# Two attention layers on one core: a gathered column that ScalarE fetches row by row, and codes of a picked column in two versions instead of seven

## The reference, cut to what matters

```python
edge_index = jnp.stack([src, dst])
x = _layernorm(x + _L0_gnn_ref(x, edge_index, ...))      # edge MLP, segment_max
x = _layernorm(x + _L1_gnn_ref(x, edge_index, ...))      # two attention layers

def _gat_conv(x, W, att_src, att_dst, bias, src, dst, n_nodes):
    h = x @ W
    a_src = h @ att_src
    a_dst = h @ att_dst
    e = a_src[src] + a_dst[dst]
    e = jnp.where(e > 0, e, NEG_SLOPE * e)
    m = jax.ops.segment_max(e, dst, num_segments=n_nodes)
    ex = jnp.exp(e - m[dst])
    denom = jax.ops.segment_sum(ex, dst, num_segments=n_nodes)
    alpha = ex / denom[dst]
    msg = alpha[:, None] * h[src]
    out = jax.ops.segment_sum(msg, dst, num_segments=n_nodes)
    return out + bias
```

## Time and profile before

| | |
|---|---|
| median of three executions | 5880.39 us (5874.37 to 5883.29) |
| profiled execution | 5872.45 us, its span 5871.2 us |
| busy share of the span | PE 84%, POOL 75%, DVE 70%, PEld 52%, ACT 45% |
| first attention layer, POOL's gathers | 2189.3 to 3896 us |
| second attention layer, POOL's gathers | 4055.9 to 5764 us |
| POOL gathers of both layers (L545) | 2712 |
| picked columns, codes, one-hot pieces of both layers | 384, 2688, 2688 |

### The profile page before, as it was taken

One profiled execution on the slowest core, in us unless ns is written; L12 is line 12 of the kernel. 1 busy time (PEld: TensorE's weight loads), 2 busy tenths in 40 slices (PEclk: granted clock), 3 DMA queues, 4 the chain that ended last, 5 costly groups with the idle time before them and its releaser, 6 DMA issues.

```text
span 5871.2 us, 119756 instructions
## 1 busy us (share of the span) xinstructions
PE 4931.6 (84%) x29429; PEld 3060.9 (52%) x29429; DVE 4098.0 (70%) x10676; ACT 2658.7 (45%) x8225; POOL 4399.4 (75%) x4585
## 2 busy tenths in 40 slices
PE   3688888888888729999999999943999999999991
PEld 2566666666666525555555555522555555555550
DVE  4344454444445448888888888864888888888886
ACT  2233333333333235555555555533555555555554
POOL 7777777777777677777777777767777777777775
PEclk6899999999999959999999999976999999999995
DMA  6677777777777724444444444432444444444442
GB/s 157 187 219 217 215 223 216 217 219 217 220 217 216 202 59 120 123 124 122 124 125 124 125 124 124 125 92 63 124 123 124 124 125 124 124 124 121 125 125 83
DMA packets 808269, 874.81 MB, mean 149 GB/s; under 512 B 133438, under 2 KB 635185, under 8 KB 807818
## 3 DMA queue, kind: packets, MB, share of 16 engines
q0 software_dynamic: 146016, 295.63, 19.7%
q1 hardware_dynamic: 390298, 361.70, 18.8%
q10 hardware_dynamic: 271504, 213.69, 13.9%
HBM read 536.74 MB, written 331.81 MB: 148 GB/s over the span
## 4 chain that ended last, share of the span: by engine, by line
POOL 51%; issue 21%; DVE 9%; PE 7%; DMA 6%; ACT 3%; DVEq 0%; POOLq 0%; SPq 0%; ACTq 0%
POOL ring_a L545 25%; POOL ring_a L485 22%; DMA ring_a<-H_table,src_i 6%; PE ps L1417 5%; DVE ring_b L1120 5%; ACT ring_a L746 2%; POOL ring_a L512 2%; POOL ad_edges L520 2%; POOL P_compact L498 1%; PE ps L1311 1%; DMA ring_a<-Q_table,src_i 1%; DVE ring_a L1074 1%; PE ps L1321 1%; DVE gz L1104 1%; DVE ring_b L1074 0%
## 5 line engine op out<-in xcount | busy, mean ns | idle before, releaser
L545 POOL DMA_INDIRECT ring_a<-H_table,src_i x2712 | 2588.2, 954 | 826.9 <-issue 755.9
L1417 PE MATMUL ps<-work,ring_a 128*128 128x390 bf16 x10752 | 1867.3, 330 | 238.5 <-DVE ring_a L1074 234.9
L485 POOL DMA_INDIRECT ring_a<-Q_table,src_i x1501 | 1432.8, 955 | 461.0 <-issue 453.0
L1417 PEld LDWEIGHTS ps<-work,ring_a 128*128 128x128 bf16 x10752 | 1015.8, 98 | 1065.2 <-DVE ring_a L1074 387.7
L1417 PE MATMUL ps<-work,ring_b 128*128 128x390 bf16 x8064 | 1407.7, 329 | 0.0
L638 ACT ACTIVATE code<-src_row,code_bias 128x128 int16<-128x128 int32 x2676 | 829.5, 389 | 1214.2 <-DVE ring_b L1074 1152.0
L1120 DVE SCALAR_TENSOR_TENSOR ring_b<-ring_b,gw,ring_a 128x129 f32<-128x129 f32 x3124 | 1092.0, 350 | 120.4 <-ACT ring_a L746 104.2
L948 DVE TENSOR_TENSOR_SCAN work<-ring_b,work,ps 128x512 f32<-128x512 bf16 x390 | 498.4, 1278 | 951.8 <-PE ps L1321 911.1
L1417 PEld LDWEIGHTS ps<-work,ring_b 128*128 128x128 bf16 x8064 | 787.0, 98 | 559.7
L746 ACT ACTIVATE ring_a<-ring_a,gw 128x129 f32<-128x129 f32 x3126 | 959.3, 390 | 0.0
L1074 DVE TENSOR_TENSOR ring_a<-code,ps 128x896 bf16<-128x896 int16 x1536 | 944.1, 615 | 1.2 <-issue 0.3
(11 more groups left out here) (267 smaller groups left out, 3625.2 us busy)
## 6 DMA issues: line engine op xcount, KB each, us to landing
run_sum<-ring_b SPq DMA_DIRECT2D x388, 520.0 KB
work<-P_compact SPq DMA_DIRECT2D x1563, 64.0 KB
ring_b<-rank_rows ACTq DMA_DIRECT2D x194, 512.0 KB, 5.2
run_max<-tab_flat ACTq DMA_DIRECT2D x194, 512.0 KB
one_rows<-H_table SPq DMA_DIRECT2D x3840, 0.5 KB
ring_a<-H_table,src_i POOLq DMA_INDIRECT x2712
src_row<-in_srcL SPq DMA_DIRECT2D x384, 64.0 KB, 3.0
ring_a<-Q_table,src_i POOLq DMA_INDIRECT x1501
```

What stands on the lines that cost most here:

```text
L485: pool.indirect_dma_start(out=q_ring[:, g % RING, j - j0, :], out_offset=None, in_=Q_table, in_offset=bass.IndirectOffsetOnAxis(ap=srcT_i[ ...
L545: pool.indirect_dma_start(out=h_ring[:, g % RING1, j - j0, :], out_offset=None, in_=H_table, in_offset=bass.IndirectOffsetOnAxis(ap=src_i[ ...
L1417: m = tensor.matmul(ps[parity][:, 0:3 * W], lhsT=hot_space[c // 4][:, c % 4, k - k0, :], rhs=split[:, k, :, :].rearrange("p s f -> p (s f) ...
```

## The change: what it does

Everything is in the two attention layers.

1. **A column by ACT.** `by_few` holds every 17th group (19, 36, ... 189; 11 a layer). One of its columns is no longer gathered by POOL. In a turn of 17 groups ACT loads the column's source numbers to `few_src` (`list_few`), then after its scaling in each of 16 groups reads two times 4 numbers into registers and issues 8 row DMAs into `few_rows` (`fetch_few`), and in the 17th moves the column to the ring (`move_few`). VectorE waits for it in the group it belongs to (`few_moved`). In one group a layer (87) both `by_row` and `by_few` apply, and POOL gathers 5 columns.
2. **Two codes for seven.** The places of blocks now stand in four PSUM banks (banks 2 to 5): bank 2 as before by TensorE, banks 3 to 5 by 21 small VectorE memsets at the start of each layer (`bf16_pair` is the bit pattern of two equal bf16 values). They hold the places 0 to 27 in units of 128, so piece c compares code c // 4 with bank c % 4, and ACT makes 2 codes instead of 7.
3. **Order.** On ACT the codes of g + 3 are made behind the row fetches, once for the group. At the layer's start ACT waits for the stored table, and VectorE's wait for `proj_tab` stands ahead of its other waits, before the memsets.

```diff
-        blocks_ps = ps[2][:, :].bitcast(BF16)[:, 0:PIECE * P].rearrange("p (k e) -> p k e", e=P)
+        blocks_ps = [ps[2 + v][:, :].bitcast(BF16)[:, 0:PIECE * P].rearrange("p (k e) -> p k e", e=P) for v in range(4)]
...
+        FEW_TURN, FEW = 17, 8
+        FEW_TURNS = (NPICK - 2) // FEW_TURN
+        by_few = [FEW_TURN * (i + 1) + 2 for i in range(FEW_TURNS)]
...
-        by_dma = [(j0, j1 - (g in picks) - (g in by_row)) for g, (j0, j1) in enumerate(groups1)]
+        by_dma = [(j0, j1 - (g in picks) - (g in by_row) - (g in by_few)) for g, (j0, j1) in enumerate(groups1)]
...
                 def code_of(g):
-                    code_row(NQPICK + layer * NPICK + picks[g])
-
+                    at = NQPICK + layer * NPICK + picks[g]
+                    scalar.wait_ge(row_landed[row_slot[at]], row_value[at])
+                    scalar.wait_ge(hot_made, at * PIECES)
+                    scalar.activation(code[:, 0, :], src_row[:, row_slot[at], :], ACT.Identity, bias=code_bias[:, 0:1])
+                    scalar.activation(code[:, 1, :], src_row[:, row_slot[at], :], ACT.Identity, bias=code_bias[:, 4:5]).then_inc(coded, 1)
+
+                def list_few(turn):
+
+                    g = by_few[turn]
+                    j = groups1[g][1] - 2 - (g in by_row)
+                    scalar.dma_start(few_src[:, :], t["srcL"][j:j + 1, :]).then_inc(few_listed, 16)
+
+                def fetch_few(turn, p):
+
+                    if p == 0:
+                        scalar.wait_ge(few_listed, 16 * (layer * FEW_TURNS + turn + 1))
+                        if layer or turn:
+                            scalar.wait_ge(few_moved, 16 * (layer * FEW_TURNS + turn))
+                    for e0 in range(p * FEW, min((p + 1) * FEW, P), 4):
+                        _, row = nc.values_load_multi_w_load_instructions(
+                            few_src[0:1, e0:e0 + 4], engines=[scalar.engine], min_val=0, max_val=NP - 1,
+                            skip_runtime_bounds_check_because="sources are numbers of nodes")
+                        for d in range(4):
+                            scalar.dma_start(few_rows[e0 + d:e0 + d + 1, :], H_table[bass.ds(row[d], 1), :]).then_inc(few_landed[layer], 16)
+
+                def move_few(turn):
+
+                    g = by_few[turn]
+                    scalar.wait_ge(few_landed[layer], 16 * P * (turn + 1))
+                    scalar.wait_ge(summed, layer * L + groups1[g - RING1][1])
+                    scalar.dma_start(h_ring[:, g % RING1, G1 - 2 - (g in by_row), :], few_rows[:, :]).then_inc(few_moved, 16)
+
+                list_few(0)
+                scalar.wait_ge(h_stored, 16 * B * (layer + 1))
...
-                        if g + 3 in picks and i == G1 - 1:
-                            code_of(g + 3)
+                    turn, p = divmod(g, FEW_TURN)
+                    if p == 0 and 1 <= turn <= FEW_TURNS:
+                        move_few(turn - 1)
+                    if p == 0 and 1 <= turn < FEW_TURNS:
+                        list_few(turn)
+                    if p >= 1 and turn < FEW_TURNS:
+                        fetch_few(turn, p - 1)
+                    if g + 3 in picks:
+                        code_of(g + 3)
...
             for layer in range(2):
+                vector.wait_ge(proj_tab, 3 * B * (layer + 1))
+                for v in range(1, 4):
+                    for k in range(PIECE):
+                        vector.memset(ps[2 + v][:, k * P // 2:(k + 1) * P // 2], bf16_pair((v * PIECE + k) * P)).then_inc(dve.up(), 1)
...
-                    vector.tensor_tensor(hot_space[c // 4][:, c % 4, 0:k1 - k0, :], code[:, c:c + 1, :].to_broadcast([P, k1 - k0, P]),
-                                         blocks_ps[:, 0:k1 - k0, :], ALU.is_equal).then_inc(hot_made, 1)
+                    vector.tensor_tensor(hot_space[c // 4][:, c % 4, 0:k1 - k0, :],
+                                         code[:, c // 4:c // 4 + 1, :].to_broadcast([P, k1 - k0, P]),
+                                         blocks_ps[c % 4][:, 0:k1 - k0, :], ALU.is_equal).then_inc(hot_made, 1)
...
+                    if g in by_few:
+                        vector.wait_ge(few_moved, 16 * (layer * FEW_TURNS + by_few.index(g) + 1))
```

More of the change, by code:

```diff
@@ L1 @@
+import struct
 from contextlib import ExitStack
@@ L36, in cut, with bf16_pair @@
     return groups
+def bf16_pair(value):
+    high = struct.unpack("<I", struct.pack("<f", float(value)))[0] >> 16
+    return struct.unpack("<f", struct.pack("<I", high * 65537))[0]
 def totals(slots, amounts):
@@ L98, in edge_network @@
         one_src, one_rows = sb("one_src", [1, P], I32), sb("one_rows", [P, W])
+        few_src, few_rows = sb("few_src", [1, P], I32), sb("few_rows", [P, W])
         x_sb = sb("x_sb", [P, NB, F])
@@ L208, in edge_network @@
         assert SHARE * (TURN - 1) >= P and all(g in picks for g in by_row) and TURN % RING1 == 0
+        FEW_TURN, FEW = 17, 8
+        FEW_TURNS = (NPICK - 2) // FEW_TURN
+        by_few = [FEW_TURN * (i + 1) + 2 for i in range(FEW_TURNS)]
+        assert FEW * (FEW_TURN - 1) >= P and all(g in picks for g in by_few)
         q_value = totals([g % RING for g in range(NG)], [16 * (j1 - j0 - (g in q_picks)) for g, (j0, j1) in enumerate(groups)])
@@ L246, in edge_network @@
         one_ready, one_landed = sem("one_ready"), [sem(f"one_rows{i}") for i in range(2)]
+        few_listed, few_moved, few_landed = sem("few_listed"), sem("few_moved"), [sem(f"few_rows{i}") for i in range(2)]
         tabs_stored, compact_zeroed, p_scattered, ranks_stored = (
@@ L1048, in vector_program @@
             for layer in range(2):
+                vector.wait_ge(proj_tab, 3 * B * (layer + 1))
+                for v in range(1, 4):
+                    for k in range(PIECE):
+                        vector.memset(ps[2 + v][:, k * P // 2:(k + 1) * P // 2], bf16_pair((v * PIECE + k) * P)).then_inc(dve.up(), 1)
                 vector.wait_ge(ad_loaded, 16 * (layer + 1))
                 vector.wait_ge(adx_loaded, 16 * (layer + 1))
-                vector.wait_ge(proj_tab, 3 * B * (layer + 1))
                 vector.wait_ge(proj_copied, 2 * B * (layer + 1))
@@ L1407, in tensor_program @@
                 for k in range(PIECE):
-                    tensor.transpose(blocks_ps[:, k, :], block_at[:, k, :], ident_b[:, :]).then_inc(blocks_put, 1)
+                    tensor.transpose(blocks_ps[0][:, k, :], block_at[:, k, :], ident_b[:, :]).then_inc(blocks_put, 1)
                 def pick(parity, added, hot):
```

## The result

The changed kernel took 5849.94 us in the median of five executions (5849.85 to 5855.10), the kernel before 5875.80 (5873.03 to 5883.29): a ratio of 0.9956, 95% interval 0.9945 to 0.9966, so 20 to 32 us faster. The forecast was 5852.7, 27.7 us under a before of 5880.39; between the two medians measured here lie 25.9 us. The profiled execution took 5855.1 us and was the slowest of its five.

What follows compares the result with a forecast made beforehand. POOL's gather rate was taken as the bound: 22 gathers at 1.259 us save 27.7 us and all other terms cost nothing, so 5880.39 - 27.7 = 5852.7 us, range 5842 to 5882.

Steps and rivals of the forecast that it cites:

- What bounds it: In the layers' steady part POOL's gather rate sets the 8.68 us a group; TensorE needs 8.2 us, VectorE 8.0.
- The gathers that go: On POOL in both layers, 22 fewer gathers at 1.259 us with gap save 27.7 us; added DMAs make none dearer.
- Will POOL be held back: POOL's wait for sums of the group three before has 7 us of room; fewer gathers use 1.26 or 2.5.
- ACT's new work: On ACT, 352 steps of 8 row fetches, 4.0 to 4.9 us each, fit 5.2 us of room: cost nothing.
- the first rival: Slow register loads push ACT's fetch step past 5.2 us, so ACT's round is the bound: 116 to about 500 slower; 13%.
- ACT becomes the bound: In the layers, ACT's own round becomes the group's time: 116 us slower, or about 500 with longest loads; chance 13%.
- SP becomes the bound: On SP's queue, each ACT issue holds up SP's for its whole 0.23 us: 350 us slower, 6230; chance 5%.
- The rest: VectorE's comparisons and wait for the moved column, some 2 us of memsets, ACT's list load and table wait: cost nothing.
- What would show each step: Signs in the trace: 2690 gathers at 1.26 us, 8.61 us a group, ACT's waits and load prices, SP still waiting.

## Why the prediction was right

**What bounds it.** Right. POOL's waits are its gap and no more, before and after, and a kernel that takes more gathers away ran down to TensorE's 8.16 us.

**The gathers that go.** Right, 22 x 1.26 us: 27.7 forecast, 25.9 measured, with 27.7 in the interval. The column left out with no replacement gave the same 0.9953 as the changed kernel on the same chip. The edge MLP's gathers were a fair row for what other DMAs do to POOL's price.

**Will POOL be held back.** Right: no wait over 0.3 us.

**ACT's new work.** The result, nothing, was right; the account behind it was wrong in its place and rough in its size. That the time came out was not luck, though: with the fetches held where the prediction had them, it was 5852.35. The prediction laid the fetches "behind the scaling and before the wait for the pieces", into a room of 5.2 us to which the shorter codes gave 1.47, and named 5.2 us as the point from which they cost. The queue starts them at the first scaling instead, 2.4 us earlier. So the point from which they cost lies, by an estimate from the round of the experiments (8.6 less 0.27, 0.1 and 0.7), near 7.5 us of fetches: 7.2 us a step was free, 10.1 was not. And the shorter codes are not what makes room for 8 rows. It also laid the fetches into idle time alone, as if ACT's queue could issue nothing while ACT works. The hint stood in the trace of before: beside ACT's first issue of the earlier trace rows, at 285.40, ACT was at work itself:

```profile
285.38 0.60 ACT L648 ACTIVATE work<-ps 128x512 f32<-128x512 f32 x1 [0.65 <-issue]
```

The size: 4.80 us at the upper end of 4.0 to 4.9, since a load took ACT 0.58 and not the 0.30 that was taken from SP, and the first issue behind a load 0.47; the others started 0.39 us apart for 0.42. By the floor that the Trainium skill gives a register load (DMA: Bandwidth & Descriptors, Latency and other measured facts) the estimate was 4.6, nearer than the row that I had preferred, though neither queue shows a floor of 600 ns: the shortest load of 4 took 0.48 us on ACT and 0.29 on SP. The two errors ran against each other, within a room wide enough for either. The prediction also made the first rival look further off than it was: the 1.9 us that two loads together would have needed is three times two median loads on SP, not six, and less than twice the two on ACT.

**ACT becomes the bound.** Not in the changed kernel; made true with 16 rows (6431) and with 12 rows and seven codes (6140), where VectorE waited for the codes as the rival had said.

**SP becomes the bound.** Out: with ACT issuing 2816 DMAs beside it, SP's row issue kept its 228 ns in the median and 234 to 235 in the mean, though two thirds of SP's 3840 ran beside one of ACT's; the longest went from 302 to 402 ns. The shared generator and its lock, of which the Trainium skill tells (Perfetto Trace Analysis, DMA Instruction — HWDGE), made no wait that shows beyond that.

**The rest.** The last fetch was to land "more than 8 us before the move". Its issue ended only 3.2 to 5.4 us before that of the move, since the move too is issued early, under the scalings of its group. It cost nothing that shows: VectorE's waits list none for the moved column.

**What would show each step.** The sign "idle time before the codes down to nothing" was wrong: it stayed at 3.02 us, since issues are not busy time and the wait still ends with VectorE's piece. Before the exponential it was 2.22 us where some 1 was expected, and a load on ACT 0.58 where 0.3 was.

## What to carry to other kernels

When one engine never rests, count what it no longer has to do at its full price, and then look at each helper's whole round, not at its idle rows: here ACT's DMA issues were in no busy time and ran beside the scalings already handed to the engine. Where in the queue such issues stand decides what they cost: behind eight ready scalings they left room even for seven codes, and behind a wait for those scalings they fitted with two codes and cost 362 us with seven. A saving on an engine that waits became waiting, to the hundredth of a us, until something else filled its round.

## What the runs showed of the hardware

- ACT's queue was ahead of the engine: the load stood behind eight scalings of 0.29 us each in the program, and the first row DMA was issued at 3008.19, beside the fourth. In all 352 steps the first load started 0.03 to 0.08 us after the first scaling. With a wait for the scalings in front, it started 0.03 us after the last one ended.
- A register load of 4 numbers took 0.30 us on SP and 0.58 on ACT in the median, but one of 12 numbers 1.73 on SP and 0.98 on ACT. On ACT the first row DMA behind a load took 0.47 us, the others 0.235.
- TensorE kept its full granted clock (1.00) in the layers whether it was busy 286 or 300 of 300 us. In the kernel with 16 rows, where it was busy 247 of 300, the mean was 0.95 (2800 to 3100 us).
